# Flamingo block: softmax denominators by reciprocals from PSUM and a shuffle, one product for maxima moved between halves, keys projected by three products

## The chip, the cores and the metric

The kernel runs on one core of a Trainium2 chip. The metric is the device time of one execution in microseconds (us); less is better. The engines are called PE (TensorE, matrix products; PEld is its loading of weights), DVE (VectorE), ACT (ScalarE), POOL (GpSimd) and SP (SyncE, which here issues the DMA transfers). Each engine takes its own instructions in order, and they wait for each other by semaphores.

## What is computed

The input is `x` (8 batches, 56 tokens, 128 features) and a context of 1500 rows of 128 per batch. A cross attention with 16 heads of 8 features comes first, then a mixture of 8 experts with the two best per token:

```python
q = (_layernorm(x) @ w_q.T)           # 16 heads of 8
k = (ctx @ w_k.T);  v = (ctx @ w_v.T)
attn = softmax(einsum('bqhd,bkhd->bhqk', q, k) * 8 ** -0.5)
x = x + tanh(g_xattn[0]) * (einsum('bhqk,bkhd->bqhd', attn, v) @ w_o.T)
# then x + tanh(g_ffn[0]) * experts(_layernorm(x)): top 2 of 8, gated by exact gelu
```

## The kernel before

The attention is cut into 16 **units**: a unit `u` is one batch and one half `h` of the heads (8 heads, as 4 pairs). A batch is units `2b` (h = 0) and `2b+1` (h = 1). Keys and queries are kept as a rounded part and a rest in the type fp32r, of which PE makes a product in one pass; a product of plain f32 is recorded as two matmul instructions.

For a unit PE makes 12 products for the row maxima (`max_scores`, L988, each into one of the three banks of `max_ps`), which DVE reduces one by one (`take_max`, L707). They are made for the unit after this one (and the first three of them for the one after that), since the maxima have to be known before the scores are. PE then makes 12 tiles of scores (`scores`, two products each, L968), which ACT exponentiates (L520), and 48 products with the values (`attend`, L1006, in two runs, q = 0 and 1), which add up in `o_ps`. The values carry a column of ones, so that row 16 of each 32 rows of `o_ps` is the softmax denominator. ACT copies `o_ps` to `o_sb` (`o_copy`, L528). In the next unit PE spreads the denominator over the 32 rows by a product with the 0/1 matrix `den_sel` (`denominators`, L1022), DVE inverts what comes out (`invert`, L733), and POOL multiplies (`normalise`, L403).

Between its runs PE has three jobs per unit (`project`): keys for two batches ahead (`k_project`, L943) and values for the next (`v_project`, L949). A unit of `attention` on PE is, in order: six maxima and six tiles of scores; job 0 (keys); the denominators of the unit before; `attend` 0; job 1 (values); the other maxima and scores; job 2; the transposition of the new maxima (`transpose_max`, L1015); `attend` 1. The order of every engine is written by hand. I call the part from the first scores to the end of job 1 the first half, and the rest, up to the first scores of the next unit, the second half. The first scores of a unit wait for the row of its maxima (`begin`, which waits for DVE's `max_rows`, L726).

The three banks of maxima go round in turns: the product of turn n waits until turn n-3 is taken (`next_bank`). The new context is loaded into `ctx_sb` (SP, L283) once the values of the last chunk of the old one are projected:

```python
sp.wait_ge(v_done, NCH * (b + 2))
sp.dma_start(ctx_sb[:, 1 - par, 0:TK], ctxT[b + 3]).then_inc(ctx_loaded[1 - par], 16)
```

Its first reader, in the next unit, is job 0, `k_project`. POOL also takes the rests of the keys (`k_rest`, L368) and spreads queries over heads (`stage`, L240). The expert stage runs from about 206 us on and isn't touched, but for one memset.

## Time and profile before

| what | value |
|---|---|
| time, median of 3 runs | 282.91 us (282.52 to 283.2) |
| the profiled execution | 283.05 us, of which the profile's span is 281.3 us |
| TensorE clock granted, mean | 1.0 of full speed |
| busy: PE, PEld | 271.1 us (96%), 220.3 us (78%) |
| busy: DVE, ACT, POOL | 216.3 us (77%), 178.9 us (64%), 98.2 us (35%) |
| chain that ended last | PE 87%, DVE 4%, ACT 4%, issue 2% |

A busy time is that in which the engine had at least one instruction under way. PE's matmuls are pipelined: one starts while the ends of the earlier ones are still modelled as running, so that the distance between starts tells the cost and not the duration. The chain of waits follows the work that ended last back to what released it.

### The profile page before, as it was taken

Reading aid. Unit: us, or ns where it says so; the run is one execution under the profiler, and the core shown is the slowest. Engines: PE = TensorE matmul, PEld = TensorE weight load, DVE = VectorE, ACT = ScalarE, POOL = GpSimd, SP = SyncE. Lnnn points to the kernel's source line nnn. Section 1 sums busy time; section 2 is a strip of 40 time slices with the busy share of each in tenths; the row PEclk is TensorE's granted clock in tenths of the full one; section 3 lists DMA queues with packets and bytes.
Section 4 is the critical chain, followed back from the end, with each engine's and each line's share of the span. In section 5 each row is a group of like instructions: output and inputs, shape, how many; then the busy total and the mean of one; then the engine's idle time right before and its main releaser. Section 6 shows DMA issues by size and latency. Waiting matters only on the chain.

```text
span 281.3 us, 8027 instructions
## 1 busy us (share of the span) xinstructions
PE 271.1 (96%) x2823; PEld 220.3 (78%) x2823; DVE 216.3 (77%) x426; ACT 178.9 (64%) x370; POOL 98.2 (35%) x114
## 2 busy tenths in 40 slices
PE   7989999999999999999999998998989999999994
PEld 3466878878878878887887887886878889999962
DVE  4679797797967978779788797788467888888771
ACT  2637776687666777678667775466718877776500
POOL 3588932232062042133205201022430855554200
PEclk9999999999999999999999999999999999999999
DMA  7397965963990990694396199300000000000001
GB/s 246 109 204 202 209 139 162 236 157 83 229 236 7 259 251 38 172 238 138 103 253 192 27 220 281 141 0 2 2 2 0 1 0 0 0 1 0 2 0 33
DMA packets 9924, 32.19 MB, mean 114 GB/s; under 512 B 2576, under 2 KB 3088, under 8 KB 9904
## 3 DMA queue, kind: packets, MB, share of 16 engines
q1 hardware_dynamic: 9472, 31.60, 44.2%
q10 hardware_dynamic: 432, 0.33, 0.4%
q8 instruction: 12, 0.20, 0.3%
q14 instruction: 8, 0.07, 0.1%
HBM read 13.26 MB, written 0.23 MB: 48 GB/s over the span
## 4 chain that ended last, share of the span: by engine, by line
PE 87%; DVE 4%; ACT 4%; issue 2%; DMA 1%; SPq 0%; POOL 0%; DVEq 0%; ACTq 0%
PE max_ps L988 16%; PE score_ps L968 15%; PE o_ps L1006 14%; PE misc_ps L949 8%; PE misc_ps L943 5%; PE score_ps L1211 3%; PE score_ps L1212 2%; PE score_ps L1213 2%; PE o_ps L1313 2%; PE misc_ps L1052 2%; PE o_ps L1211 2%; PE o_ps L1212 2%; PE o_ps L1213 2%; DVE part_max L707 2%; PE score_ps L943 2%
## 5 line engine op out<-in xcount | busy, mean ns | idle before, releaser
L707 DVE TENSOR_REDUCE part_max<-max_ps 112x1 f32<-112x512 f32 (+1 forms) x192 | 117.9, 670 | 31.2 <-PE max_ps L988 29.4
L520 ACT ACTIVATE probs<-score_ps 128x448 f32<-128x448 f32 x188 | 88.0, 547 | 13.2 <-PE score_ps L968 13.0
L988 PE MATMUL max_ps<-kx,qx 96*112 96x512 f32 (+1 forms) x192 | 79.7, 421 | 1.1 <-DVE qx L240 0.5
L968 PEld LDWEIGHTS score_ps<-qx,kx 104*128 104x128 f32 x376 | 63.8, 188 | 9.1 <-issue 3.2
L968 PE MATMUL score_ps<-qx,kx 104*128 104x224 f32 x376 | 67.6, 276 | 0.0
L1006 PE MATMUL o_ps<-probs,v_sb 128*32 128x112 f32 (+1 forms) x1536 | 44.4, 261 | 0.8 <-ACT probs L520 0.8
L988 PEld LDWEIGHTS max_ps<-kx,qx 96*112 96x112 f32 x192 | 33.7, 176 | 7.0 <-issue 4.6
L1006 PEld LDWEIGHTS o_ps<-probs,v_sb 128*32 128x32 f32 (+1 forms) x1536 | 36.7, 110 | 3.0 <-ACT probs L520 1.0
L368 POOL TENSOR_TENSOR k_low<-k_full,k_high 128x512 fp32r<-128x512 f32 (+1 forms) x21 | 26.3, 1253 | 32.4 <-ACT k_full L502 32.1
L403 POOL TENSOR_TENSOR o_norm<-o_sb,inv_den 128x112 f32 (+1 forms) x15 | 6.6, 440 | 76.6 <-DVE inv_den L733 76.6
L514 ACT ACTIVATE v_sb<-misc_ps 128x512 f32<-128x512 f32 x24 | 14.4, 601 | 28.0 <-PE misc_ps L949 28.0
L949 PE MATMUL misc_ps<-wv_sb,ctx_sb 128*128 128x128 f32 x192 | 27.0, 283 | 0.4 <-ACT v_sb L514 0.2
L949 PEld LDWEIGHTS misc_ps<-wv_sb,ctx_sb 128*128 128x128 f32 x192 | 23.9, 191 | 3.8 <-issue 2.4
L430 POOL TENSOR_TENSOR kx<-gu_sb,kx 128x512 fp32r<-128x512 f32 x16 | 21.1, 1331 | 8.9 <-ACT kx L608 8.5
L612 ACT ACTIVATE v_sb<-score_ps 128x448 f32<-128x448 f32 x29 | 15.5, 548 | 5.4 <-PE score_ps L1213 5.0
L943 PE MATMUL misc_ps<-ctx_sb,wk_sb 128*128 128x512 f32 (+1 forms) x36 | 18.0, 581 | 0.0
L898 DVE TENSOR_TENSOR kx<-probs,kx 128x448 fp32r<-128x448 f32 x24 | 17.4, 765 | 0.0
L240 POOL TENSOR_TENSOR qx<-q_parts,head_mask 96x448 fp32r<-96x448 f32 x15 | 13.9, 931 | 7.9 <-PE score_ps L968 7.0
L733 DVE RECIPROCAL inv_den<-max_ps 128x112 f32<-128x112 f32 x17 | 14.6, 857 | 2.1 <-PE max_ps L1022 1.7
L634 ACT ACTIVATE kx<-probs 128x448 fp32r<-128x448 f32 x24 | 13.7, 578 | 3.3 <-DVE probs L893 2.8
L499 ACT ACTIVATE k_high<-misc_ps 128x512 fp32r<-128x512 f32 (+1 forms) x18 | 10.6, 588 | 5.4 <-PE misc_ps L943 5.4
L528 ACT ACTIVATE o_sb<-o_ps 128x112 f32<-128x112 f32 x16 | 4.2, 264 | 13.6 <-PE o_ps L1006 13.6
(192 smaller groups left out, 381.8 us busy)
## 6 DMA issues: line engine op xcount, KB each, us to landing
kx<-k_high SPq DMA_DIRECT2D x60, 187.5 KB, 5.4
kx<-k_low SPq DMA_DIRECT2D x30, 187.5 KB, 5.2
ctx_sb<-in_ctxT SPq DMA_DIRECT2D x7, 750.0 KB, 5.7
gu_sb<-in_guT SPq DMA_DIRECT2D x8, 512.0 KB, 5.6
dn_sb<-in_dnT SPq DMA_DIRECT2D x8, 256.0 KB, 5.8
ctx_sb<-in_ctxT SPq DMA_DIRECT2D x2, 256.0 KB, 4.0
kx<-k_high SPq DMA_DIRECT2D x4, 123.5 KB, 2.3
kx<-k_high SPq DMA_DIRECT2D x4, 64.0 KB, 2.0
```

The costliest lines, as they stand in the source:

```text
L368: nc.gpsimd.tensor_tensor(k_low[:, par, start:start + size], k_full[:, start:start + size], k_high[:, par, start:start + size].bitcast(f32 ...
L430: nc.gpsimd.tensor_tensor(weight_parts[:, kind, par, 1, :], weights_of(kind, e), weight_parts[:, kind, par, 0, :].bitcast(f32), ALU.subtra ...
L520: nc.scalar.activation(probs[:, (KT * h + t) % 8, :], bank[:, 0:SC // 2], ACT.Exp, scale=SCALE).then_inc(exp_done, 1)
L612: nc.scalar.activation(gelu_sb[:, par, j, :], banks[j % len(banks)][:, 0:TOK], ACT.Gelu).then_inc(gelu_ready, 1)
L707: nc.vector.reduce_max(part_max[:, p, c:c + 1], max_ps[0:PC, bank, 0:size], AX.X).then_inc(max_taken, turns)
L733: nc.vector.reciprocal(inv_den[:, PC * h:PC * h + PC], max_ps[:, bank, 0:PC]).then_inc(max_taken, 1)
L898: nc.vector.tensor_tensor(hact_parts[:, j, 1, :], hact[:, j, :], hact_parts[:, j, 0, :].bitcast(f32), ALU.subtract).then_inc(hact_ready, 1)
L943: nc.tensor.matmul(bank[:, 0:size], wk_sb[:, :], ctx_sb[:, par, start:start + size], start=True, stop=True).then_inc(k_done, 1)
L949: last = nc.tensor.matmul(misc_ps[:, 128 * k:128 * k + 128], ctx_sb[:, par, 128 * t:128 * t + 128], wv_sb[:, :], start=True, stop=True)
L968: last = nc.tensor.matmul(bank[0:m, GC * g:GC * g + GC], kx[0:KR, 2 * par + h, g, 128 * t:128 * t + m], qx[0:KR, par, 2 * h + g, :], start ...
L988: nc.tensor.matmul(max_ps[0:PC, bank, 0:size], qx[0:MR, par, 2 * h + p // 2, PC * (p % 2):PC * (p % 2) + PC], kx[0:MR, slot, p // 2, start ...
L1006: last = nc.tensor.matmul(o_ps[32 * j:32 * j + 32, PC * h:PC * h + PC], v_sb[0:m, par, t, VP * p:VP * p + 32], probs[0:m, (KT * h + t) % 8 ...
```

## The change

1. *Denominators.* The product with `den_sel` and its matrix are gone. DVE takes the reciprocal straight from `o_ps` (all 128 rows of the half, with no use for most), after four of the unit's maxima (`MID`), and later spreads row 16 over its 32 rows by a shuffle. PE's `attend` 0 now waits until the copy and the reciprocal of the unit before are made, since both halves of `o_ps` lie in one bank. POOL's `normalise` waits for the shuffle. In the last unit the copy by ACT is gone and DVE multiplies out of `o_ps`.
2. *Maxima.* The turn that the denominators had is used by the tenth product for maxima, which moves from the second half ahead of `attend` 0; its turn counts double.
3. *Keys.* For batches 2 to 7 `k_project` (one f32 product) becomes `k_product3`: three products in fp32r, of the high and low parts of weights and context. POOL makes the parts (`split_context`: a cast and a subtraction for each chunk of 512 columns), in one buffer `ctx_parts`, so that a split waits for the product before. POOL's loop is written out.
4. *Around it.* Two of the four memsets of the ones rows of `kx` (POOL) become two DMAs (SP); the memset of `combT` moves to after the last keys and into `ctx_parts`; a memset of half of `o_ps` (DVE) comes into the first maxima.

```diff
+        ctx_parts = sb("ctx_parts", [D, 2, CK], f32r)
+        wk_parts = sb("wk_parts", [D, 2, D], f32r)
...
+            sp.wait_ge(kx_ones, 1)
+            for slot in (2, 3):
+                sp.dma_start(kx[MR:KR, slot, :, :].bitcast(f32), kx[MR:KR, 0, :, :].bitcast(f32)).then_inc(ones_moved, 16)
...
-            ones_rows(2)
-            ones_rows(3)
+            def split_context(i, par, n):
+                made = NCH * batch(i, par) + n
+                start, size = chunk(n)
+                src = ctx_sb[:, par, start:start + size]
+                pool.wait_ge(k_done, 2 * NCH + made)
+                nc.gpsimd.tensor_copy(ctx_parts[:, 0, 0:size], src).then_inc(ctx_high, 1)
+                pool.wait_ge(ctx_high, made + 2)
+                nc.gpsimd.tensor_tensor(ctx_parts[:, 1, 0:size], src, ctx_parts[:, 0, 0:size].bitcast(f32), ALU.subtract
+                                        ).then_inc(ctx_split, 1)
+            def split_first(i, par):
+                pool.wait_ge(ctx_loaded[par], 16 * (i + 2))
+                split_context(i, par, 0)
...
+            def reciprocals(u, h, done=None):
+                dve.wait_ge(o_norm_ready, u + FIRST_NORM - 1)
+                if done is None:
+                    dve.wait_ge(o_saved, u + 2)
+                else:
+                    dve.wait_ge(pv_done, done)
+                nc.vector.reciprocal(inv_den[:, PC * h:PC * h + PC], o_ps[:, PC * h:PC * h + PC]).then_inc(den_taken, 1)
+            def spread_inverse(u, h):
+                half = inv_den[:, PC * h:PC * h + PC]
+                nc.vector.stream_shuffle(half, half, [DEN_ROW] * 32).then_inc(inv_ready, 1)
...
-                for n in range(RUN):
+                for n in range(MID):
                     take_max(ring(u, n), n % 3, AHEAD + n)
-                invert(u - 1, 1 - h, ring(u, DEN), DEN % 3)
-                for n in range(RUN + AHEAD, UM):
+                reciprocals(u - 1, 1 - h)
+                for n in range(MID, RUN):
+                    take_max(ring(u, n), n % 3, AHEAD + n)
+                dve.wait_ge(den_taken, u + 1)
+                take_max(ring(u, SEVENTH), SEVENTH % 3, AHEAD + RUN, turns=2)
+                spread_inverse(u - 1, 1 - h)
+                for n in range(AHEAD + RUN + 1, UM):
...
+            def k_product3(i, par, n):
+                size = chunk(n)[1]
+                pe.wait_ge(ctx_split, NCH * batch(i, par) + n + 2)
+                for w, c in ((0, 0), (0, 1), (1, 0)):
+                    last = nc.tensor.matmul(misc_ps[:, 0:size], wk_parts[:, w, :], ctx_parts[:, c, 0:size],
+                                            start=w + c == 0, stop=w == 1)
+                last.then_inc(k_done, 1)
...
+                if q == 0:
+                    pe.wait_ge(o_saved, u + 1)
+                    pe.wait_ge(den_taken, u + 1)
```

PE, one h = 1 unit of the loop before, from the last maxima of its first six to the third maxima of the second half:

```order
L988 MATMUL max_ps<-kx,qx 112x476
L943 MATMUL misc_ps<-ctx_sb,wk_sb 128x476
L1022 MATMUL max_ps<-o_sb,den_sel 128x112
L1006 MATMUL o_ps<-probs,v_sb 32x112 x24
L949 MATMUL misc_ps<-wv_sb,ctx_sb 128x128 x4
L988 MATMUL max_ps<-kx,qx 112x512
L968 MATMUL score_ps<-qx,kx 128x224 x2
L988 MATMUL max_ps<-kx,qx 112x512
L968 MATMUL score_ps<-qx,kx 128x224 x2
L988 MATMUL max_ps<-kx,qx 112x476
```

The same place after the change:

```order
L1053 MATMUL max_ps<-kx,qx 112x476
L1005 MATMUL misc_ps<-ctx_parts,wk_parts 128x476 x3
L1053 MATMUL max_ps<-kx,qx 112x512
L1074 MATMUL o_ps<-probs,v_sb 32x112 x24
L1012 MATMUL misc_ps<-wv_sb,ctx_sb 128x128 x4
L1053 MATMUL max_ps<-kx,qx 112x512
L1033 MATMUL score_ps<-qx,kx 128x224 x2
L1053 MATMUL max_ps<-kx,qx 112x476
```

The denominators' product has become one for maxima, the keys' product three, and the second half has one product for maxima less.

POOL, one batch of the loop before (`qx` is `stage`, `k_low` is `k_rest`, `o_norm` is `normalise`):

```order
L240 TENSOR_TENSOR qx<-q_parts,head_mask 96x448
L368 TENSOR_TENSOR k_low<-k_full,k_high 128x512
L240 TENSOR_TENSOR qx<-q_parts,head_mask 96x448
L368 TENSOR_TENSOR k_low<-k_full,k_high 128x512
L368 TENSOR_TENSOR k_low<-k_full,k_high 128x476
L403 TENSOR_TENSOR o_norm<-o_sb,inv_den 128x2x56
L403 TENSOR_TENSOR o_norm<-o_sb,inv_den 128x2x56
```

The same after the change, up to the second split:

```order
L406 CAST ctx_parts<-ctx_sb 128x512
L408 TENSOR_TENSOR ctx_parts<-ctx_sb,ctx_parts 128x512
L244 TENSOR_TENSOR qx<-q_parts,head_mask 96x448
L406 CAST ctx_parts<-ctx_sb 128x512
L408 TENSOR_TENSOR ctx_parts<-ctx_sb,ctx_parts 128x512
L370 TENSOR_TENSOR k_low<-k_full,k_high 128x512
L421 TENSOR_TENSOR o_norm<-o_sb,inv_den 128x2x56
L406 CAST ctx_parts<-ctx_sb 128x476
L408 TENSOR_TENSOR ctx_parts<-ctx_sb,ctx_parts 128x476
L244 TENSOR_TENSOR qx<-q_parts,head_mask 96x448
```

Three pairs of a cast and a subtraction have come in, the first of them ahead of everything else of the batch.

## Rows read from the trace of the kernel before

**Rows 1.** The page, busy time of each engine.

```profile
PE 271.1 (96%) x2823; PEld 220.3 (78%) x2823; DVE 216.3 (77%) x426; ACT 178.9 (64%) x370; POOL 98.2 (35%) x114
```

**Rows 2.** Chain of waits in batch 3: start, us, engine and work.

```profile
95.85 0.43 PE score_ps L968 x2
...
98.52 0.86 PE misc_ps L943 x2
...
107.06 0.41 PE max_ps L988
107.47 0.44 PE score_ps L968 x2
...
111.15 1.29 PE o_ps L1006 x48
112.43 1.09 PE misc_ps L949 x8
...
117.36 1.25 PE o_ps L1006 x48
...
119.03 0.43 PE score_ps L968 x2
```

**Rows 3.** Timeline of DVE in the same h = 1 unit.

```profile
107.51 3.68 DVE L707 TENSOR_REDUCE part_max<-max_ps 112x1 f32<-112x512 f32 x6 [0.21 <-PE max_ps L988]
111.19 0.86 DVE L733 RECIPROCAL inv_den<-max_ps 128x112 f32<-128x112 f32 x1
113.79 1.85 DVE L707 TENSOR_REDUCE part_max<-max_ps 112x1 f32<-112x512 f32 x3 [1.75 <-PE max_ps L988]
...
118.24 0.62 DVE L726 TENSOR_TENSOR qx<-max_ps,pair_mask 8x448 fp32r<-8x448 f32 x1
```

**Rows 4.** Timeline of ACT, second half of this unit.

```profile
114.06 2.79 ACT L520 ACTIVATE probs<-score_ps 128x448 f32<-128x448 f32 x6
```

**Rows 5.** Timeline of PE, experts: first and last of 18 fp32r products, back to back.

```profile
218.19 0.36 PE L1211 MATMUL score_ps<-k_high,kx 128*128 128x448 f32 x1
...
221.63 0.36 PE L1213 MATMUL score_ps<-kx 128*128 128x448 f32 x1
```

**Rows 6.** Groups of POOL: busy us, mean ns, idle before.

```profile
L368 POOL TENSOR_TENSOR k_low<-k_full,k_high 128x512 fp32r<-128x512 f32 x14 | 18.0, 1282 | 8.1 <-ACT k_full L502 7.8 <-DVE neg_max_parts L717 0.3
...
L436 POOL CAST kx<-gu_sb 128x512 fp32r<-128x512 f32 x3 | 1.8, 611 | 7.4 <-PE score_ps L968 3.5 <-DVE xn L682 2.0 <-DVE neg_max_parts L717 1.9
```

**Rows 7.** SP's timeline, the context's five loads (L283), and the transfers from 110 to 125.

```profile
113.70 0.34 SPq L283 DMA_DIRECT2D ctx_sb<-in_ctxT  x1
...
DMA to landing us min/median/max: 5.2/5.7/7.2
...
ctx_sb<-in_ctxT SPq DMA_DIRECT2D x1, 750.0 KB, 6.3
```

**Rows 8.** Timeline of POOL and chain of waits around the first unit.

```profile
23.96 2.43 POOL L368 TENSOR_TENSOR k_low<-k_full,k_high 128x512 fp32r<-128x512 f32 x2 [0.30 <-DVE neg_max_parts L717]
...
28.93 0.86 PE misc_ps L943 x2
```

**Rows 9.** Timeline of PE, unit 12.

```profile
175.04 0.26 PE L1015 MATMUL max_ps<-ident,neg_max_parts 112*8 112x112 f32 x1 [0.84 <-DVE part_max L707]
```

**Rows 10.** Timelines of DVE and PE, unit 14.

```profile
188.46 3.60 DVE L707 TENSOR_REDUCE part_max<-max_ps 112x1 f32<-112x512 f32 x6 [0.30 <-PE max_ps L988]
...
192.75 1.78 DVE L707 TENSOR_REDUCE part_max<-max_ps 112x1 f32<-112x512 f32 x3
...
193.28 1.36 PE L1006 MATMUL o_ps<-probs,v_sb 128*32 128x112 f32 x48
```

**Rows 11.** Timelines of DVE and PE, end of the attention.

```profile
204.87 0.99 DVE L812 TENSOR_TENSOR kx<-xnT,kx 128x336 fp32r<-128x336 f32 x1 [3.21 <-ACT kx L602]
206.09 0.86 DVE L733 RECIPROCAL inv_den<-max_ps 128x112 f32<-128x112 f32 x1 [0.23 <-PE max_ps L1022]
206.98 0.28 DVE L818 TENSOR_TENSOR o_norm<-o_sb,inv_den 128x112 f32<-128x112 f32 x1
...
207.31 1.13 PE L1137 MATMUL misc_ps<-wo_sb,o_norm 128*112 128x128 f32 x8 [0.37 <-DVE o_norm L818]
```

More of the change, by code:

```diff
@@ L130, in flamingo_block @@
         comb_parts = sb("comb_parts", [RT, NR, 2, E], f32r)
-        combT = sb("combT", [ROWS, TOK], f32r)
+        combT = ctx_parts[:, 0, 0:TOK]
         out_sb = xn
@@ L417, in body @@
                 normalise(i, par, 0)
-                normalise(i, par, 1)
-            with pool.Fori(0, B // 2 - 1) as i:
-                body(i, 0)
-                body(i, 1)
+            for b in range(B - 2):
+                i, par = divmod(b, 2)
+                split_first(i, par)
+                first_unit(i, par)
+                if b:
+                    normalise(*divmod(b - 1, 2), 1)
+                second_unit(i, par)
             pool.wait_ge(scores_done, KT * (NU - 4) + 1)
             stage(B - 1, 1, 1)
+            normalise(2, 1, 1)
             normalise(3, 0, 0)
@@ L441, in select @@
                 nc.gpsimd.tensor_copy(expert_now[:, par, :], bc(row_mask[:, e].unsqueeze(1), [ROWS, 128])).then_inc(select_ready, 1)
+            pool.wait_ge(k_done, NCH * B)
+            serial(nc.gpsimd.memset(combT[:, :].bitcast(f32), 0.0))
             pool.wait_ge(ffn_loaded, 16 * (1 + 2 * E))
@@ L768, in _ @@
                 take_max(n, n % 3, n, first=True)
+                if n == 7:
+                    dve.wait_ge(q_full_saved, 1)
+                    nc.vector.memset(o_ps[:, PC:2 * PC], 1.0).then_inc(o_saved, 1)
             negate_max(0, UM)
@@ L788, in last_but_one @@
             def last_but_one(u):
-                for n in range(DEN):
+                for n in range(MID):
                     take_max(ring(u, n), n % 3, AHEAD + n)
-                invert(u - 1, 1, ring(u, DEN), DEN % 3)
-                for n in range(DEN + 1, TAIL):
+                reciprocals(u - 1, 1)
+                dve.wait_ge(den_taken, u + 1)
+                for n in range(MID, RUN):
+                    take_max(ring(u, n), n % 3, AHEAD + n, turns=2 if n == RUN - 1 else 1)
+                spread_inverse(u - 1, 1)
+                for n in range(RUN + 1, TAIL):
                     take_max(ring(u, n), n % 3, AHEAD + n - 1)
@@ L956, in begin @@
                 if par == 0 and h == 1:
-                    pe.wait_ge(kx_ones, 4)
+                    pe.wait_ge(kx_ones, 2)
+                if par == 1 and h == 0:
+                    pe.wait_ge(ones_moved, 32)
             def scores(i, par, h, t, banks=None):
@@ L1017, in transpose_max @@
                                  ident[0:PC, 0:PC], start=True, stop=True).then_inc(rows_done, 1)
-            def denominators(u, h, turn, bank):
-                pe.wait_ge(o_saved, u + 2)
-                next_bank(turn)
-                nc.tensor.matmul(max_ps[:, bank, 0:PC], den_sel[:, :], o_sb[:, PC * h:PC * h + PC], start=True, stop=True
-                                 ).then_inc(max_done, 1)
             def project(i, par, h, c):
@@ L1118, in attention @@
                 job(i, par, h, 0)
-                denominators(u - 1, 1 - h, ring(u, DEN), DEN % 3)
+                max_scores(*u1, AHEAD + RUN, ring(u, SEVENTH), SEVENTH % 3, turns=2)
                 attend(i, par, h, 0)
                 job(i, par, h, 1)
-                for n in range(RUN + AHEAD, UM):
+                for n in range(AHEAD + RUN + 1, UM):
                     max_scores(*u1, n, ring(u, n - 2), (n - 2) % 3)
-                    scores(i, par, h, n - AHEAD)
+                    scores(i, par, h, n - AHEAD - 1)
                 for n in range(AHEAD - 1):
                     max_scores(*u2, n, ring(u, LATER + n), (LATER + n) % 3)
-                    scores(i, par, h, KT - AHEAD + n)
+                    scores(i, par, h, KT - AHEAD - 1 + n)
+                scores(i, par, h, KT - 2)
                 scores(i, par, h, KT - 1)
@@ L1165, in last_scores, with last_max, keep_warm @@
                     scores(3, 1, h, t, last_banks if h else None)
-            def last_max(n, turn):
-                max_scores(3, 1, 1, n, ring(NU - 2, turn), turn % 3)
-            def keep_warm(times, bank=o_ps):
+            def last_max(n, turn, turns=1):
+                max_scores(3, 1, 1, n, ring(NU - 2, turn), turn % 3, turns=turns)
+            def keep_warm(times, bank):
                 for _ in range(times):
-                    nc.tensor.matmul(bank[:, 0:128], den_sel[:, :], den_sel[:, :], start=True, stop=True)
+                    nc.tensor.matmul(bank[:, 0:128], ident[:, :], ident[:, :], start=True, stop=True)
             for t in range(RUN):
-                last_max(AHEAD + t, t)
+                last_max(AHEAD + t, t, 2 if t == RUN - 1 else 1)
                 last_scores(0, t, t + 1)
-            denominators(NU - 3, 1, ring(NU - 2, RUN), RUN % 3)
             for t in range(RUN, 8):
```

72 lines of the change are left out of this document (37 added, 35 removed).

## The prediction, made before the changed kernel ran

> **What bounds the kernel now.** I read the busy times first: PE has work under way for 96% of the span [rows 1]. So I went to the chain of waits, and there to one batch of the loop. It lies on PE nearly throughout. An h = 0 unit takes 107.47 - 95.85 = 11.62 us from first scores to first scores, an h = 1 unit 119.03 - 107.47 = 11.56 us [rows 2]. The reader should look for two places where PE isn't the limit. The maxima's product ahead of the first scores stands for 0.41 us [rows 2] where its 512 columns cost some 0.22, and DVE's `max_rows` ends at 118.24 + 0.62 = 118.86, just ahead of the scores at 119.03 [rows 2, 3]: PE waits about 0.2 us per unit for DVE. And DVE, once it has the second half's first product at 113.79, works without a gap up to that end; its free time is the 1.75 us ahead of 113.79 [rows 3]. So PE bounds the first half, and in the second half DVE is only 0.2 us behind, or ahead.
>
> I write S for a unit's first scores. In the h = 1 unit `attend` 0 starts at S + 3.68, job 1 ends at 112.43 + 1.09 = 113.52 = S + 6.05, and the second half takes 119.03 - 113.52 = 5.51 us [rows 2].
>
> **The products.** Three kinds of work change on PE.
>
> *Keys.* The f32 product of 512 columns takes 0.86 us on the chain [rows 2]. Of fp32r products, 17 steps between starts take 221.63 - 218.19 = 3.44 us, 0.202 us per 448 columns [rows 5]; with 64 columns more, in proportion, 0.23, and three of them 0.69. A key chunk saves about 0.16 us, 0.5 us per batch. VectorE: DVE Perf Modes, section on the TRN2 errata, in the Trainium skill, gives a matmul max(60, 6 + columns) cycles at 2.4 GHz. By that page, as an estimate, three products take 0.65 us and the sum would be 0.9 us lower over 18 chunks; the row has the issue between products in it, and I go by the row.
>
> *Denominators.* Nothing else stands between a keys' product and `attend` 0, and 0.21 us lie there: 98.52 + 0.86 = 99.38 against an `attend` 0 at S + 3.74, 99.59, in the h = 0 unit (98.52 is S + 2.67 in both, and the h = 1 one of 476 columns starts `attend` 0 0.06 earlier) [rows 2]. The maxima's product that comes here costs the same, 0.22. So the first half is no shorter by this, and the second half, which loses a product, is 0.22 us shorter.
>
> **First half.** By PE alone `attend` 0 would come at S + 3.55 (less 0.16 for keys). But now it waits for the reciprocal. With the stall of 0.2 us gone the first maxima come after S - 0.22 and DVE starts at S + 0.23. Four reductions at 3.68/6 = 0.61 us and a reciprocal of 0.86 us [rows 3] end at S + 3.54, and with the signal PE starts `attend` 0 at about S + 3.62. That leaves 0.09 us saved on average. Reading `o_ps` instead of `max_ps` I cost at nothing, both being PSUM. DVE's later work (two reductions, the moved one, the shuffle) ends at S + 3.54 + 1.83 + 0.28 = S + 5.65, and the second half's first product is not there before S + 6.2: half a microsecond of cover. The shuffle has no row. Its bounds are the multiplication on 128x112, 0.28 us, and the reciprocal of the same shape, 0.86 us [rows 3, 11]; I take 0.28, as it calculates nothing. At 0.86 the cover is just used up and a unit in the loop loses under 0.1 us.
>
> **Second half.** PE alone: 5.51 - 0.2 (stall) - 0.22 = 5.09 us in h = 1 units, and with a keys' product in job 2 4.93 in h = 0 units. DVE's chain from its first product to the next scores was 119.03 - 113.79 = 5.24 us after a start 0.27 us behind job 1; one reduction less makes 5.51 - 0.61 = 4.90. ACT's six exponentials end at 114.06 + 2.79 = 116.85, 3.33 us behind job 1, and `attend` 1 waits for them; it starts now at 117.36 [rows 2, 4], 3.84 behind, and will be at 3.46 to 3.62. So nothing new waits, but the h = 0 half has three engines within 0.1 us. I take 5.09 and 4.95.
>
> A batch is then shorter by 2 x 0.09 + 0.42 + 0.56, some 1.15 us; over six batches 6.8 us.
>
> **The context's chain.** This is what may eat it. The load starts 0.18 us behind job 1 of an h = 1 unit (113.70 against 113.52) and lands 5.2 to 7.2 us after, with a median of 5.7 of five [rows 2, 7]. Before, keys were needed 5.51 + 2.67 = 8.18 us behind job 1, well after the landing. Now POOL first splits: a cast of 0.61 and a subtraction of 1.28 us [rows 6], with three signals of some 0.07 us 2.1. So the products are ready at L + 2.27 behind job 1 for a landing L, and PE is there at 5.09 + 2.67 = 7.76. It waits for all of L above 5.49. The five loads: 5.2 costs nothing, 5.7 0.2, 7.2 1.7, the one at 113.70 had 6.3 and costs 0.8 [rows 7], and the fifth lies between minimum and median, 0.1. Together 2.8 us. Queued behind the waiting product are the moved maxima and `attend` 0, so nothing of it comes back. The other two chunks of a batch have 5 us between products, against 2 of splitting and 1.3 or 0.9 of other POOL work; I cost them at nothing. POOL's load grows by 3 x 1.9 us in a batch of 22; it was 35% busy [rows 1].
>
> The Trainium skill, GPSIMD Engine Reference, section Key points, warns that POOL shares its SBUF interfaces with VectorE and contends with its instructions that have two SBUF inputs or a 2-port mode. DVE's long instructions in this stage read PSUM, so by that rule the splits keep their length.
>
> **The ends.** In the first unit the load was issued long before, but POOL is done with `k_low` only at 26.39 [rows 8]; weights, then the split, give about 29.2 where the keys' product started at 28.93: +0.35. The memset into `o_ps` lies in a row of DVE's reductions there: +0.2. The two ones-row DMAs stand in SP's queue where it was idle and are needed two units later: nothing. Units 12 and 13 have no keys. Their second halves were held by DVE (a wait of 0.84 us on `part_max` in unit 12 [rows 9]), so they gain the whole reduction in one case, -0.6, and -0.4 in the other, where a job fills the wait. Unit 14 loses: DVE works there without a gap from 188.46 [rows 10]. The tenth product waited for the fifth reduction only; with the reciprocal ahead of that reduction it comes 0.86 later, and `attend` 0, formerly at 193.28, some 0.6 later, as do the three reductions of 192.75: +0.6. Unit 15 loses one small product, -0.15. In the last unit the reciprocal seems to gain a copy and a product, but DVE is at work until 204.87 + 0.99 = 205.86 before it, so it starts 0.2 earlier than at 206.09, and the shuffle with its signal takes 0.34 before the multiplication [rows 11]: +0.1.
>
> **Sum**: -6.8 + 2.8 + 0.35 + 0.2 - 0.6 - 0.4 + 0.6 - 0.15 + 0.1 = -3.9. The profiled execution took 283.05 us, 0.14 above the median shown; 283.05 - 3.9 = 279.15, so 279.2 us.
>
> **The rivals.**
>
> *The splits are in time.* If landings are like the shortest, or PE comes to the keys later than I think, the 2.8 us are not lost: 276.3. With the shuffle at 0.28 and units a bit shorter, 275. For it speaks that four of the five landings are close to the limit; against it that all but one were over 5.49 or near it.
>
> *The context's chain is longer, and the kernel slower.* Without its waits the change is worth 6.7 us; over five loads that is 1.34 us each, and it is used up at L = 6.8. Should all loads land like the slowest, at 7.2, each costs 1.7, together 8.6: 283.05 - 6.7 + 8.6 = 285.0. For it: the landing is a transfer of 750 KB beside the keys' moves, and one took 7.2. If the landing is counted from the end of the 0.34 us of issue and not from its start, the forecast itself is 1.7 us higher. Against it: the median is 5.7.
>
> *DVE becomes the bound.* With the shuffle at 0.86 us, 0.6 more in unit 14, 0.6 at the end, and 0.1 in 12 units: 279.2 + 2.4 = 281.6. For it: DVE is 0.2 us from the bound in each second half. Against: half a microsecond of cover.
>
> *No effect.* The three products are no quicker than one, and the swap of denominators for maxima gains only the stall: 279.2 + 18 x 0.16 = 282.1, with small waits at three engines it is 283. The 0.202 us of [rows 5] speak against it.
>
> **How the numbers follow.** Forecast 0.45 (its own range 277.8 to 280.6), in time 0.25, context's chain slower 0.12, DVE 0.11, no effect 0.07. The range of 275.2 to 283.0 leaves out the worst part of the slower case and a little below. A measurement of this kernel tells 0.2% from no change, 0.6 us, so between 282.3 and 283.5 it is the same. Faster: 0.45 + 0.25 + 0.10 + 0.02 = 0.82; same 0.06; slower 0.12.
>
> **What would show it.** Right: no L1022, h = 1 first scores without the 0.2 us stall; keys' product of three steps in 0.7 us; PE waiting for POOL's `ctx_parts` at job 0 of h = 0 units only, by L - 5.5; `attend` 0 starting at S + 3.6 with DVE's reciprocal as the last released. Wrong: a DVE wait inside the second half; splits above 2.1 us; PE waiting for POOL at jobs of other chunks; landings that have moved.

## The result and the profile after

Over 20 executions each, the changed kernel took 281.37 us (median; 279.5 to 285.56) and the one before 283.0 us (282.52 to 283.87): a ratio of 0.9934, 95% interval 0.9912 to 0.9957. It is faster by 0.66%, where the forecast of 279.2 us said 1.4%. Here and below ratios leave out the slow executions (of this series three of the changed kernel, 284.48 us and more), while medians are of all. The profiled execution took 280.42 us, 2.6 us less than that of before, with a span of 278.7 us.

Two things have to be explained: the profiled execution gained 2.6 us and not 3.9, and the median gained only 1.6. The spread is the first thing to see: from end to end it was 1.35 us, and has become 6.

Busy times of the changed kernel, from its page:

```profile
PE 265.4 (95%) x2807; PEld 218.9 (79%) x2807; DVE 216.7 (78%) x460; ACT 178.6 (64%) x369; POOL 125.2 (45%) x148
```

PE has 5.7 us less under way than in [rows 1], and POOL, with the splits, 27 us more. The chain of waits through the same two units as in [rows 2] (start, us, engine and work):

```profile
95.18 0.42 PE max_ps L1053
95.61 0.22 PE score_ps L1033 x2
...
98.14 0.70 PE misc_ps L1005 x3
...
106.29 0.42 PE max_ps L1053
106.71 0.22 PE score_ps L1033 x2
...
109.24 0.64 PE misc_ps L1005 x3
109.88 0.23 PE max_ps L1053
110.19 1.36 PE o_ps L1074 x48
111.55 1.09 PE misc_ps L1012 x8
...
114.22 0.86 PE score_ps L1033 x6
...
115.29 0.89 PE misc_ps L1012 x8
...
117.63 0.42 PE max_ps L1053
```

From one maxima's product ahead of first scores to the next, the h = 0 unit now takes 106.29 - 95.18 = 11.11 us and the h = 1 unit 117.63 - 106.29 = 11.34; before it was 11.62 and 11.56 [rows 2]. So a batch is shorter by 0.73 us, where I had put 1.15. The keys' product is 0.70 us, as forecast. But the product at the head of a unit (the one for maxima ahead of its first scores) still stands for 0.42 us. DVE in the same h = 1 unit, timeline, to be held against [rows 3]:

```profile
106.75 2.44 DVE L734 TENSOR_REDUCE part_max<-max_ps 112x1 f32<-112x512 f32 x4 [0.52 <-PE max_ps L1053]
109.11 0.85 DVE L763 RECIPROCAL inv_den<-o_ps 128x112 f32<-128x112 f32 x1
...
111.58 0.28 DVE L768 STREAM_SHUFFLE inv_den<-inv_den 128x112 f32<-128x112 f32 x1
...
116.80 0.62 DVE L753 TENSOR_TENSOR qx<-max_ps,pair_mask 8x448 fp32r<-8x448 f32 x1
```

The four reductions, the reciprocal and the shuffle stand where they were expected; the shuffle took 0.28 us. DVE's `max_rows` now ends at 116.80 + 0.62 = 117.42, before the next head starts on PE at 117.63, and the head still takes its 0.42 us. So what the head takes above 0.22 us is no wait for DVE.

There had been such a wait, one row further on. The first scores' weights are `qx`, which `max_rows` writes; PEld loads them so, before and after:

```profile
118.98 0.30 PEld L968 LDWEIGHTS score_ps<-qx,kx 104*128 104x128 f32 x2 [0.26 <-issue]
```

```profile
117.65 0.43 PEld L1033 LDWEIGHTS score_ps<-qx,kx 104*128 104x128 f32 x2
```

Before, the load began 0.12 us behind the end of `max_rows` (118.86 [rows 3]) and 0.36 behind the head's start (118.62), and the first scores stood for 0.43 or 0.44 us [rows 2]. Now it begins 0.02 us behind the head's start, and the first scores take 0.22. In unit 13 of the kernel before, `max_rows` ended 0.16 us behind the head's start and not 0.24, and the first scores took 0.27.

The second half lost one of its six products for maxima. Before, job 2 of the h = 1 unit:

```profile
116.27 0.89 PE misc_ps L949 x8
```

From the end of job 1 to job 2 it was 116.27 - 113.52 = 2.75 us [rows 2], and now 115.29 - 112.64 = 2.65 (112.64 = 111.55 + 1.09). The product that went gave 0.10 us and not its 0.22: the last three tiles of scores now follow each other without one between them and take 0.86 us, where a tile between two products for maxima takes 0.22.

The chain of waits at the first unit, and at the batch that was released latest in the loop:

```profile
21.03 6.76 DMA ctx_sb<-in_ctxT
...
29.85 0.96 PE misc_ps L1005 x3
```

```profile
67.23 6.17 DMA ctx_sb<-in_ctxT
...
73.45 0.62 POOL ctx_parts L406
...
74.14 1.29 POOL ctx_parts L408
...
75.47 0.97 PE misc_ps L1005 x3
```

In the first unit the load of the third context took 6.76 us and the keys' product started at 29.85, where it had been 28.93 [rows 8]. In the batch of unit 4 the chain runs from a landing of 6.17 us over POOL's two splits of 0.62 and 1.29 us into the keys. Such a product takes 0.97 us behind a wait and 0.70 without one, so a wait costs PE 0.27 us above its length. The five loads of the loop landed after 5.5, 6.2, 5.0, 5.6 and 5.8 us, and the units that read them are longer than an undisturbed h = 0 unit of 11.11 us by 0.04, 0.69, 0, 0.11 and 0.28.

Timelines of DVE and PE in unit 14, the place of [rows 10]:

```profile
185.84 2.45 DVE L734 TENSOR_REDUCE part_max<-max_ps 112x1 f32<-112x512 f32 x4 [0.76 <-PE max_ps L1053]
188.21 0.84 DVE L763 RECIPROCAL inv_den<-o_ps 128x112 f32<-128x112 f32 x1
189.09 1.25 DVE L734 TENSOR_REDUCE part_max<-max_ps 112x1 f32<-112x512 f32 x2
```

```profile
189.83 0.48 PE L1053 MATMUL max_ps<-kx,qx 96*112 96x512 f32 x1 [1.33 <-DVE part_max L734]
...
191.24 1.36 PE L1074 MATMUL o_ps<-probs,v_sb 128*32 128x112 f32 x48
...
194.96 1.27 PE L1074 MATMUL o_ps<-probs,v_sb 128*32 128x112 f32 x44 [0.84 <-ACT probs L548]
```

PE stands idle for 1.33 us there, because the fifth reduction comes behind the reciprocal.

Laid end to end, the two profiled executions differ so:

| stretch | before | after | difference |
|---|---|---|---|
| to the head of unit 1 | 37.52 | 38.22 | +0.70 |
| to the head of unit 14 | 150.49 | 147.17 | -3.32 |
| to its second `attend` | 8.99 | 9.57 | +0.58 |
| to the projection of the output | 10.31 | 9.96 | -0.35 |
| the rest | 73.99 | 73.78 | -0.21 |

### The profile page after: what moved, and what is told of

Its sections match the earlier page's. It is cut to its first block, busy times and chain, and to the rows that moved or that the text cites. A ratio compares the mean times of both kernels' runs of the same rounds, so it can differ in the third digit from the quotient of the medians.

```text
span 278.7 us, 8055 instructions
## 1 busy us (share of the span) xinstructions
PE 265.4 (95%) x2807; PEld 218.9 (79%) x2807; DVE 216.7 (78%) x460; ACT 178.6 (64%) x369; POOL 125.2 (45%) x148
## 4 chain that ended last, share of the span: by engine, by line
PE 74%; ACT 6%; DVE 6%; DMA 6%; SPq 3%; issue 2%; POOL 2%; DVEq 0%; ACTq 0%
PE max_ps L1053 14%; PE o_ps L1074 13%; PE score_ps L1033 13%; PE misc_ps L1012 7%; PE misc_ps L1005 5%; DMA ctx_sb<-in_ctxT 5%; SPq L251 3%; PE score_ps L1269 3%; ACT probs L548 3%; PE score_ps L1271 2%; PE score_ps L1270 2%; PE o_ps L1371 2%; PE o_ps L1269 2%; PE o_ps L1271 2%; PE o_ps L1270 2%
## 5 line engine op out<-in xcount | busy, mean ns | idle before, releaser
L1074 PE MATMUL o_ps<-probs,v_sb 128*32 128x112 f32 (+1 forms) x1536 | 45.2, 261 | 1.3 <-ACT probs L548 0.8
L1074 PEld LDWEIGHTS o_ps<-probs,v_sb 128*32 128x32 f32 (+1 forms) x1536 | 37.5, 110 | 7.5 <-ACT probs L548 5.1
L406 POOL CAST ctx_parts<-ctx_sb 128x512 fp32r<-128x512 f32 (+1 forms) x18 | 10.8, 600 | 46.3 <-DMA ctx_sb<-in_ctxT 29.9
L408 POOL TENSOR_TENSOR ctx_parts<-ctx_sb,ctx_parts 128x512 fp32r<-128x512 f32 (+1 forms) x18 | 22.5, 1250 | 1.4
L1005 PE MATMUL misc_ps<-ctx_parts,wk_parts 128*128 128x512 f32 (+1 forms) x54 | 15.6, 397 | 1.5 <-POOL ctx_parts L408 1.4
L421 POOL TENSOR_TENSOR o_norm<-o_sb,inv_den 128x112 f32<-128x112 f32 x15 | 6.3, 421 | 20.4 <-DVE inv_den L768 20.4
L763 DVE RECIPROCAL inv_den<-o_ps 128x112 f32<-128x112 f32 x17 | 14.4, 847 | 0.2 <-ACT o_sb L556 0.2
```

Source lines behind the costliest of these rows:

```text
L408: nc.gpsimd.tensor_tensor(ctx_parts[:, 1, 0:size], src, ctx_parts[:, 0, 0:size].bitcast(f32), ALU.subtract).then_inc(ctx_split, 1)
L1005: last = nc.tensor.matmul(misc_ps[:, 0:size], wk_parts[:, w, :], ctx_parts[:, c, 0:size], start=w + c == 0, stop=w == 1)
L1074: last = nc.tensor.matmul(o_ps[32 * j:32 * j + 32, PC * h:PC * h + PC], v_sb[0:m, par, t, VP * p:VP * p + 32], probs[0:m, (KT * h + t) % 8 ...
```

## Experiments

My explanation from these rows: (1) the 0.2 us at a unit's head is PE's own and no wait; (2) keys gain nothing in h = 1 units, since the reciprocal ends later than PE arrives; (3) the rest of the loss is waits for the context's landing. The rival to (1) is my forecast's wait for DVE, and to (3) a cause that the profiled execution doesn't show, since the other executions are slower than it.

**The changed kernel again, and with less split.** On one chip, the changed kernel unaltered:

> The changed kernel again, beside the kernel before on one chip, to have the granted clock of every execution of both. Theory A (the spread of the changed kernel's times, 279.5 to 285.6, comes from TensorE's granted clock): executions at a clock of 0.998 and more lie at 279.5 to 281, those at 0.992 to 0.994 two or three us above, and time and clock fall on one line; the kernel before stays at 1.0 and within 1.3 us. Theory B (the spread comes from the landing of the context's loads, for which PE now waits): times spread by 3 us or more at one and the same clock.

It took 283.2 us (12 executions, 280.07 to 288.14; ratio 0.9948, 0.9918 to 0.9977). The clock sorts the times as theory A there says, but not alone: three executions at 0.998 to 1.0 took 280.07, 280.26 and 282.74 us, so theory B holds for a part of the spread. The profiled execution, at 282.03 us, showed what that of the first series had not. Its windows around unit 14 (the window, its length, us of PE busy, number of products, granted clock, DMA's share, GB/s), and PE's timeline there:

```profile
190.00:191.00 1.00, 1.00 (x5) 0.80 0.00 0
191.00:192.00 1.00, 1.00 (x8) 0.50 0.08 16
...
193.00:194.00 1.00, 1.00 (x32) 0.50 0.00 0
```

```profile
189.93 0.49 PE L1053 MATMUL max_ps<-kx,qx 96*112 96x512 f32 x1 [1.34 <-DVE part_max L734]
...
191.92 2.35 PE L1074 MATMUL o_ps<-probs,v_sb 128*32 128x112 f32 x48
...
196.62 1.36 PE L1074 MATMUL o_ps<-probs,v_sb 128*32 128x112 f32 x48 [0.84 <-ACT probs L548]
```

Behind the idle 1.34 us PE is granted 0.5 of its clock, the 1.2 GHz level of its two, for 0.4 + 3 us, and then 2.4 GHz again. `attend` 0 takes 2.35 us, in the first execution 1.36. From the product behind the wait to the second `attend` it is 196.62 - 189.93 = 6.69 us against 194.96 - 189.83 = 5.13: 1.56 us for one fall of the clock, of the 1.61 between the two profiled executions (282.03 and 280.42). The Trainium skill, TensorE: Matmul & The Clock Gate, section HAM oscillation — how this bites in real kernels, describes falls of this kind behind waits for DMA; the waits in its example are longer than this one. The trace agrees that a fall comes behind idle time of PE, and here 1.34 us of it stood ahead.

The mean granted clock, which is on record for every execution, then sorts the executions. The three series of the changed kernel have 33: 12 with 0.996 or more (9 of the first series: 279.5 to 281.04), 13 with 0.992 to 0.994 (first series 280.75 to 283.54), 8 with 0.986 to 0.988 (first series 284.48 to 285.56). The kernel before is always at 0.996 or more. My explanation had nothing of this. I added (4), which the expectations below call theory G: the reciprocal ahead of the fifth reduction makes the idle time, and the idle time the fall.

*Keys in f32*, no split at all:

```diff
-                split_context(i, par, 1)     # and 0 and 2
...
-                for w, c in ((0, 0), (0, 1), (1, 0)):
-                    last = nc.tensor.matmul(misc_ps[:, 0:size], wk_parts[:, w, :], ctx_parts[:, c, 0:size],
+                if n == 0:
+                    pe.wait_ge(ctx_loaded[par], 16 * (i + 2))
+                k_project(batch(i, par) + 2, par, n, misc_ps)
```

> The changed kernel with the keys by one f32 product each and no splits on POOL; the denominators and the maxima as changed. Theory 1 (the three products are worth 0.16 us a chunk, and PE's waits for the first chunk's split eat them): 18 x 0.16 = 2.9 us come back and the waits of 2.2 us in the loop and 0.9 us at the first unit go, so 280.0 to 280.7 where the clock is full, the same as the changed kernel. Rival (the gain of the whole change is the keys'): 282 or more. If the fp32r products are what lowers the granted clock, this kernel stays at 0.998 and more in all executions, and its median lies below the changed kernel's.

281.93 us (12 executions; 0.9955, 0.9932 to 0.9978): the same as the changed kernel beside it, as expected. *Only the first chunk of a batch in f32*, so that the split isn't on the way from landing to product (PE's part of the edit; POOL's split of that chunk goes too):

```diff
+                if n == 0:
+                    pe.wait_ge(ctx_loaded[par], 16 * (i + 2))
+                    k_project(batch(i, par) + 2, par, 0, misc_ps)
+                    return
```

> The changed kernel, but the first chunk of each batch's keys goes by one f32 product straight from the context, as before, and only the second and third are split. Theory 1: the waits for the split vanish (2.2 + 0.9 us) and 6 x 0.16 = 1.0 us is given back, so 278.3 (277.8 to 279.0) at full clock. Rival (PE would have waited at that place anyway, for the landing itself or for another engine): 280 or more.

280.37 us (280.17 to 281.0; 0.9899, 0.9881 to 0.9918), all six at a clock of 0.992 or 0.993. I had expected 278.3 at full clock; with the 1.56 us of a fall taken off it is 278.8. The spread is 0.8 us, where the unaltered kernel beside it has 8. So the waits on the context are part of the trouble, and they vary from one execution to the next.

**A product of full width between tiled ones.** The values' products of `attend` are 32 columns of the array wide, all others use its full width. One small product (128 x 32, its output is used by nothing) was put into `attend` 0 of 14 units, once in its middle and once behind it:

```diff
+            def small(u):
+                pe.wait_ge(max_taken, ring(u, MID) + 1)
+                nc.tensor.matmul(max_ps[:, 1, 0:32], ident[:, :], ident[:, 0:32], start=True, stop=True)
...
-                attend(i, par, h, 0)
+                attend(i, par, h, 0, between=small)   # the other kernel: small(u) behind it
```

> The changed kernel with one useless small product (a 128x128 f32 matrix on 32 columns, into a free bank of the maxima) in the middle of the first run of the value products, in each of 14 units. My prediction took 0.2 us ahead of a unit's first scores for a wait for DVE; but in the changed kernel DVE is done 0.2 us before PE gets there, and the 0.42 us of the maxima's product stand unchanged. Theory S (it costs PE 0.2 us by itself to go from the value products, which write 32 of 128 rows each, to a product over the whole width): this kernel is slower than the changed one by the small product's own 0.1 and by 0.2 or more per unit, 4.2 us or more in 14 units. Rival (the 0.2 us hang on the unit's head: its waits and its branch): only the own cost of 1.4 us. Compare with the next run, in which the same product stands at an existing seam.

> The changed kernel with the same useless small product per unit as in the last run, but between the first run of value products and the values' projection, where the width changes anyway. In the run with it in the middle of the value products the stretch grew by 0.47 to 0.54 us per unit. Theory S (0.2 us or more for each change of width): here a unit grows only by the product's own 0.1 to 0.2 us, so 282 to 283 us at a clock of 0.993 to 1.0. Rival (the product itself costs 0.5 us wherever it stands): 287 to 288.

They took 288.39 and 285.12 us, one execution each with a clock of 0.993; of the second I had expected 282 to 283. Chain of waits, the same h = 1 unit, product in the middle:

```profile
113.54 0.78 PE o_ps L1076 x24
114.33 0.34 PE max_ps L1172 x2
114.66 0.71 PE o_ps L1076 x24
115.38 1.09 PE misc_ps L1012 x8
```

The product behind `attend` 0:

```profile
111.96 1.36 PE o_ps L1074 x48
113.32 0.34 PE max_ps L1170 x2
113.66 0.97 PE misc_ps L1012 x8
```

The small product is 0.34 us in both. In the middle, the two halves of `attend` take 0.78 + 0.71 = 1.49 us and the values' projection 1.09; behind it 1.36 and 0.97. So one more pair of changes between tiled and full width costs 1.49 + 1.09 - 1.36 - 0.97 = 0.25 us, and by the whole times (288.39 - 285.12) / 14 = 0.23. Single executions of this kernel can differ by more than that, so the units without a wait are the better measure: from head to head an h = 1 unit takes 11.82 us with the product in the middle, 11.56 with it behind and 11.34 without it, an h = 0 unit 11.58, 11.33 and 11.11. The pair of changes is worth 0.25 us in both kinds, and the product itself 0.22. This supports (1): the head of a unit takes 0.42 instead of 0.22 us because it follows `attend` 1, as the values' projection takes 1.09 behind `attend` 0 and 0.89 elsewhere. I had read the longer duration of the head as a wait. The Trainium skill, TensorEngine Tiling (Array Packing), section Key Properties, says that a change of the tiling mode drains TensorE; it gives no price, and these runs show 0.25 us for a pair of changes.

**The reciprocal behind all six reductions of unit 14.** Only there:

```diff
-                for n in range(MID):
-                    take_max(ring(u, n), n % 3, AHEAD + n)
+                for n in range(RUN):
+                    take_max(ring(u, n), n % 3, AHEAD + n, turns=2 if n == RUN - 1 else 1)
...
-                for n in range(MID, RUN):
-                    take_max(ring(u, n), n % 3, AHEAD + n, turns=2 if n == RUN - 1 else 1)
```

> The changed kernel, but in unit 14 alone the reciprocal comes behind all six reductions, as the inversion did before, and not behind four. Theory G (the reciprocal ahead of the fifth reduction makes PE wait 1.3 us in unit 14; this costs 0.6 us by itself, and in many executions the granted clock falls to 0.5 for some 3.4 us right behind that wait, for 1.7 us more): the time at full clock is 279.8, the dip at that place is gone in every execution, the executions at 0.992 become rare, the median falls to 279.8 to 280.5. Executions with another dip behind a wait for the context may remain. Rival (the clock falls by chance or heat, wherever PE is denser): as many executions at 0.992 as before, median 281 to 283.

281.2 us (six executions, 279.41 to 281.88; 0.991, 0.9882 to 0.9938). Timelines of DVE and PE in unit 14:

```profile
187.08 3.61 DVE L734 TENSOR_REDUCE part_max<-max_ps 112x1 f32<-112x512 f32 x6 [0.75 <-PE max_ps L1051]
190.60 0.85 DVE L763 RECIPROCAL inv_den<-o_ps 128x112 f32<-128x112 f32 x1
```

```profile
190.19 0.48 PE L1051 MATMUL max_ps<-kx,qx 96*112 96x512 f32 x1 [0.44 <-DVE part_max L734]
...
195.54 0.69 PE L1072 MATMUL o_ps<-probs,v_sb 128*32 128x112 f32 x20 [0.63 <-ACT probs L548]
```

The six reductions are in one piece again, PE's idle time there is 0.44 us, and from the first reduction to the second `attend` it is 195.54 - 187.08 = 8.46 us, against 194.96 - 185.84 = 9.12 before the edit: 0.66 us back, which undoes the +0.58. The clock was 0.998 or more in five executions of six. The median missed the 279.8 to 280.5 that I had expected. In the profiled execution, at 280.97 us, two loads landed after 7.0 and 6.9 us, and PE waited 2.9 us in all for the context's splits; the fastest, at full clock too, took 279.41. Unit 2 of this execution stood idle for 1.41 us, and there the clock did not fall.

*Useless products in the wait instead*, with the reciprocal where the change had it:

```diff
+            pe.wait_ge(max_taken, ring(NU - 2, 3) + 1)
+            keep_warm(5, max_ps[:, 0, :])
```

> The changed kernel, with the wait of unit 14 left as it is but five useless products (128x128, f32, some 1.1 us) in it, into a bank of the maxima that is free by then. Theory G, its second half (the clock falls because PE stands idle): no dip there, executions at 0.998 and more at 280.2 to 280.8, nothing gained by the wait itself. Rival (the clock falls for what comes behind the wait, or by chance): the same share of executions with a dip of 0.008 as for the changed kernel.

281.74 us (five executions, 279.19 to 287.79), clocks of 1.0 three times, 0.994 and 0.988. The 0.994 was profiled, and its fall wasn't in unit 14 but in unit 2, from 54.1 on, behind a wait of 1.39 us for the context (windows, columns as above):

```profile
54.00:55.00 1.00, 0.96 (x3) 0.56 1.00 240
```

So a wait for the context can be followed by a fall too, and the same wait in the run above was not. Whether the useless products help in unit 14 this run doesn't tell apart: two of its five executions have a clock under 0.996, and only one of them was profiled.

**The two edits together.** *Late reciprocal with the first chunk in f32*:

> The changed kernel with both repairs: the first chunk's keys by one f32 product, and the late reciprocal in unit 14. The run with the first repair alone gave 280.37 with a dip to 0.992 in all six executions. Theory G and theory 1 together: 280.4 - 1.7 (dip) - 0.6 (wait) = 278.1 (277.6 to 278.6), clock 0.998 and more in all, spread under 1 us, ratio to the kernel before 0.981 to 0.984. Rival (the dips are not from that wait): 279.7 and up.

279.28 us (279.12 to 279.53; 0.9857, 0.984 to 0.9874), where I had expected 278.1. The repair of unit 14 gave what it should: from the head of unit 14 to the end the profiled execution is 2.3 us shorter than with the first chunk in f32 alone. But it was 1.0 us longer up to the head of unit 1, and I have no cause for that. *Late reciprocal with all keys in f32*, which leaves of the change only the denominators and maxima:

> The changed kernel with the late reciprocal in unit 14 and the keys by one f32 product each, without splits: of the change, the denominators and the maxima alone, without both kinds of wait. Theory 1: against the version with both repairs (279.28 us) it lacks 12 chunks by three products, 12 x 0.16 = 1.9 us, so 281.2 (280.7 to 281.6), at a clock of 0.996 and more in all executions. Then the denominators and maxima are worth 2 us and the keys, freed of their waits, about as much again. Rival (the keys' products bring nothing, all the gain of the repaired version is in the rest): 279.3.

279.28 us too (279.14 to 280.36; 0.9874, 0.9852 to 0.9895). All nine executions have a clock of 0.997 or more. I had expected 281.2 of it: the three products for keys, 12 in the one and none in the other, brought nothing between these two kernels. The profiled executions show a gain of 0.17 us in each h = 0 unit of the loop (11.38 and 11.21), none in the h = 1 units, and a head of unit 1 that comes 0.8 us later with the splits. Its chain of waits, the h = 1 unit:

```profile
105.54 0.42 PE max_ps L1045
...
108.48 0.80 PE misc_ps L992 x2
...
109.51 1.29 PE o_ps L1066 x48
...
116.88 0.42 PE max_ps L1045
```

This unit takes 116.88 - 105.54 = 11.34 us with a keys' product of 0.80 us, exactly as long as with the three products of 0.64 (109.24, in the changed kernel's chain above). There the next product ends at 109.88 + 0.23 = 110.11, `attend` 0 starts only at 110.19, and it takes 1.36 us instead of the 1.29 here: 0.08 + 0.07 us, all that the keys had saved. Of what `attend` 0 waits for, DVE's reciprocal ended last, at 109.11 + 0.85 = 109.96. The profile names another, ACT, at the load of `attend` 0's weights:

```profile
110.19 1.12 PEld L1074 LDWEIGHTS o_ps<-probs,v_sb 128*32 128x32 f32 x48 [0.50 <-ACT probs L548]
```

ACT's exponentials had ended at 109.81, and where they do hold `attend` (unit 14, 194.90 to 194.96) the load starts 0.06 us behind them. So the reciprocal fits better, but no run moved the one without the other: that half of (2) is argued and not shown; that the h = 1 units gain nothing from the keys is shown. The h = 0 unit takes 11.39 us in this kernel and 11.11 in the changed one, 0.28 of 0.33 us kept.

*The changed kernel once more*, one execution:

> The changed kernel once more, one look, as a further sample of the loads' landings and the clock: a wait for the first unit's split of some 0.9 us, loads landing 5.2 to 7.2 us after their issue, 280 to 286 us.

281.33 us with a clock of 0.992, and granted 0.5 from 189.9 to 193.3.

**The context's load by itself.** The last way to keep three products: SP issues no move of keys until the context has landed (with the late reciprocal; the loop on SP written out):

```diff
                     sp.dma_start(ctx_sb[:, 1 - par, 0:TK], ctxT[b + 3]).then_inc(ctx_loaded[1 - par], 16)
+                    sp.wait_ge(ctx_loaded[1 - par], 16 * (i + 2 + par))
```

> The changed kernel with the late reciprocal in unit 14; besides, SP waits in each batch until the new context has landed before it issues the twelve moves of keys (its loop is written out for that). Theory 1 (PE waits for the landing because the load shares the DMA rings with the moves): the loads land in 3.5 to 4.5 us instead of 5.2 to 7.3, POOL's first split is done before PE gets to it, PE has no wait for it in the loop, and unless the later moves are missed the time is 278.5 to 279.3 with little spread. Rival (the landing is a matter of the load's own size): landings as before, and no gain. If the moves come too late, PE waits for the keys at the maxima, and the time is over 281.

278.53 us (278.16 to 279.3; 0.983, 0.981 to 0.985), as expected. The landings of the five loads, in the changed kernel and in this one:

```profile
DMA to landing us min/median/max: 5.0/5.6/6.2
```

```profile
DMA to landing us min/median/max: 4.1/4.1/4.5
```

Alone, 750 KB land in 4.1 to 4.5 us; beside the keys' moves in 5.0 to 6.2 (and up to 7.2 in [rows 7]). No wait for a split is left in the loop.

*And the two ones-row DMAs behind the keys' moves of batch 1*, not right behind the third context's load:

```diff
-            sp.wait_ge(kx_ones, 1)      # ahead of move_unit(1, 0)
-            for slot in (2, 3): ...
             move_unit(1, 0)
             move_unit(1, 1)
+            sp.wait_ge(kx_ones, 1)
+            for slot in (2, 3): ...
```

> The version load_alone with one thing more: the two DMAs of the ones rows stand behind the keys' moves of batch 1 and not right behind the context's load. Theory (the ones rows' DMAs share the queues with the third context's load and make it land late, 6.3 to 6.8 us after its start where the kernel before had 5.4): the landing comes back to about 5.4, the first keys' product starts up to 0.9 us earlier, and the head of unit 2 with it: 277.6 to 278.2 us where load_alone had 278.5. Rival (the landing is late from the keys' moves that are still under way, or PE isn't waiting for it any more): no change, 278.3 to 278.8, first keys' product where it was. Third: the ones rows are now late for unit 2 and PE waits there, above 279.

278.19 us (277.78 to 278.77; 0.9814, 0.9798 to 0.983), the best, and at the upper end of what I had expected. Its interval overlaps that of the version before it, so that the 0.3 us are not shown by the times. The mechanism is, in POOL's timelines; with the DMAs right behind the load:

```profile
28.61 0.61 POOL L407 CAST ctx_parts<-ctx_sb 128x512 fp32r<-128x512 f32 x1 [0.50 <-DMA ctx_sb<-in_ctxT]
```

With them behind:

```profile
27.66 0.61 POOL L407 CAST ctx_parts<-ctx_sb 128x512 fp32r<-128x512 f32 x1
```

The load landed 6.7 us after its start in the one and 5.3 in the other, and POOL's wait of 0.50 us for it is gone. In the twelve profiled executions with the DMAs right behind it this load landed after 5.9 to 7.0 us, in the two without, of the kernel before and of this one, after 5.4 and 5.3. It isn't free: the first load of the loop, now issued while the transfer of `wo` is under way, landed after 5.8 us instead of 4.5, and unit 2 is 0.25 us longer.

## Why the forecast was half right

**Right: direction, range, and most rows.** The keys' product at 0.70 us, the shuffle at 0.28, four reductions and a reciprocal, splits of 0.61 and 1.28, and unit 14 (+0.6 forecast, +0.58 measured) came as put. Units 12 and 13 gave 0.45 and 0.12 us, 0.6 together where I had 1.0.

**The step that failed** is the second half, "5.51 - 0.2 (stall) - 0.22 = 5.09 us". It came to 118.05 - 112.64 = 5.41 us in h = 1 units, and to 5.22 in h = 0 units instead of 4.95. Both terms were mis-sized. The stall was read from the head's 0.41 us, and the head is still 0.42: the excess is the change from the 32-column products of `attend` 1 to full width. The product for maxima was priced at its 0.22 us of the chain, and taking it out gave 0.10. A stall was there, but in the row behind the head, the first scores' 0.44 us; its end falls into the first half, which is shorter by 0.12 us in h = 1 units and 0.23 in h = 0 units, instead of 0.09 in each. So a batch gained 0.73 us and not 1.15. The kernel with the denominators and maxima alone has batches of 22.73 us against 23.18, 0.45 for two units, where the stall and the product had been put at 0.84 in the second halves. Over the six batches the difference is 2.5 us of the forecast.

**The first half of h = 1 units.** "That leaves 0.09 us saved": the keys' shorter product brought nothing there, 11.34 us with and without it. PE alone was as I had put it, S + 3.40. But since the head kept its length, DVE began at S + 0.04 and not at S + 0.23; the reciprocal ended at S + 3.25 and not at S + 3.54, and `attend` 0 started at S + 3.48, where I had 3.62.

**The context's chain** was right as a mechanism, and even its rule "It waits for all of L above 5.49" held: for the loads of 5.5, 6.2, 5.0, 5.6 and 5.8 us it gives 0.01, 0.71, 0, 0.11 and 0.31, measured 0.04, 0.69, 0, 0.11 and 0.28. In the execution with landings of 7.0 and 6.9 us it gives 2.9 in the loop, and 3.0 were measured. That is in part luck, since PE came to the keys later than the 7.76 us behind job 1 that the rule was worked out from (5.41 + 2.53 = 7.94), and a wait costs 0.27 us above its length. The waits were 1.1 us against 2.8 because these landings were shorter than those of before. The first unit was worse: up to the head of unit 1 my terms add up to -0.09 - 0.56 + 0.35 + 0.2 = -0.10 us, and it was +0.70. There I had priced POOL's readiness and not the landing; the ones-row DMAs, which I put at nothing, stand right behind that load.

**Not foreseen: the clock.** I gave unit 14 its 0.6 us and stopped there. An idle PE of 1.3 us costs the wait and then, in many executions, 1.56 us more. Executions with a clock of 0.996 or more, with the reciprocal ahead of the fifth reduction and behind the sixth: 12 of 33 and 5 of 6 for the changed kernel, 0 of 6 and 4 of 4 with the first chunk in f32, 3 of 12 and 5 of 5 with all keys in f32. With the two versions with the load alone this makes 15 of 51 and 23 of 24. That the order of the reciprocal brings the falls is shown by this; that it does so by the idle time is argued from the rows. The nine executions of the first series without a fall have a median of 280.42 us, 2.6 below before, and the whole series 1.6 below. The medians of the three clock classes in the first series (280.42, 282.79, 284.95) lie 2.4 and 2.2 us apart, more than the 1.56 of the fall in the rows. I can't say what the rest is; slow landings, which bring waits and falls together, would do it, but no profile shows that.

In sum, for the profiled execution: 2.5 us less than forecast in the batches, 0.7 in the first unit beyond that, and 0.4 in units 12 and 13; against it 1.7 us less of waits and 0.5 less at the end. So -2.6 instead of -3.9 us, with the waits hiding part of the first error, and the clock took 1 us of the median. Of the rivals, "in time" was nearer for the landings than my own case, and "no effect" for the keys: 0.16 us of PE's time brought nothing in a unit where `attend` 0 couldn't start earlier. In the best version (the last above) the splits gain 1.1 us from unit 1 to unit 14 (147.42 us without them, 146.31 with), and 0.7 of it is given back ahead of unit 1 (37.37 us without them, 38.06 with).

## What to carry to other kernels

A product that takes longer than the same product elsewhere isn't waiting only because another engine ends nearby: look for the same excess at a place with no such neighbour, above all where the products change between a part and the full width of the array. Look at the weight load as well: a product that waits for its weights stands longer in the chain, with no idle time of PE. A product's share of the chain is not what its removal gives. When an instruction is put ahead of a reduction that PE waits for, find the place where that reduction has no slack (here the unit without jobs) and order it otherwise there. Before a transfer gets a consumer that is tighter by 2 us, take its landing's worst and not its median, and ask what else is issued beside it.

## What the runs showed of the chip

- A change from products 32 columns wide to full width and back costs PE about 0.25 us (11.82 against 11.56 us and 11.58 against 11.33 a unit); it stands in the duration of the work that follows, not as idle time.
- First scores whose weights were loaded 0.36 us behind the head's start stood for 0.43 or 0.44 us, with the load at 0.02 to 0.07 us they stood for 0.22.
- PE idle for 1.3 us in unit 14 came with a mean clock under 0.996 in 36 of 51 executions; the four of these that were profiled show 3.4 us at 1.2 GHz right behind it. Idle 1.4 us in unit 2 was followed by it once and once not; what decides stays open.
- A load of 750 KB landed in 4.0 to 4.5 us alone (5.8 once, issued while a transfer of 256 KB was under way), and in 5.0 to 7.2 us beside other moves of the same queue.
